# Swapping PSUM banks each step in latent attention, and a second expert unit ahead of the routes

## The reference

```python
logits = jnp.einsum('bsh,eh->bse', x, classifier_w)
probs = jax.nn.softmax(logits, axis=-1)
_, idx = jax.lax.top_k(probs + e_score_correction_bias, TOP_K)
rw = jnp.take_along_axis(probs, idx, axis=-1) * SCALE
w_full = jnp.sum(jax.nn.one_hot(idx, total) * rw[..., None], axis=-2)
act = jax.nn.silu(g) * u                      # g, u: each expert's gate and up products
expert_out = jnp.einsum('bsei,ehi->bseh', act, down_w)
out = jnp.einsum('bse,bseh->bsh', w_full[..., :n_routed], expert_out)

q_big = _apply_rope(jnp.einsum('bshk,hkq->bshq', q_hk, w_kc_q), sin_q, cos_q)
q_r = jnp.einsum('bshq,hqr->bhsr', q_big, W_qr)
k_r = jnp.einsum('bld,hdr->bhlr', kv_r, W_kr)
attn = jax.nn.softmax(jnp.einsum('bhsr,bhlr->bhsl', q_r, k_r), axis=-1)
ctx_c = jnp.einsum('bhsl,bld->bhsd', attn, kv_r)
```

## Time and profile before

| | |
|---|---|
| time, median of 3 runs | 873.98 us (868.6 to 875.28) |
| profiled execution | 870.11 us |
| its span, first to last instruction | 868.2 us |
| mean granted TensorE clock | 0.967 of full |
| TensorE matmul busy | 773.2 us (89%) |
| VectorE busy | 649.5 us (75%) |
| GpSimd busy | 553.4 us (64%) |
| ScalarE busy | 400.4 us (46%) |
| experts' first gate matmul | 191.70 us |
| latent attention's first query matmul | 377.37 us |
| last layer's first matmul | 769.4 us |

### The profile page before, as it was taken

One profiled execution on the slowest core, in us unless ns is written; L12 is line 12 of the kernel. 1 busy time (PEld: TensorE's weight loads), 2 busy tenths in 40 slices (PEclk: granted clock), 3 DMA queues, 4 the chain that ended last, 5 costly groups with the idle time before them and its releaser, 6 DMA issues. The chain is left out here.

```text
span 868.2 us, 14841 instructions
## 1 busy us (share of the span) xinstructions
PE 773.2 (89%) x4808; PEld 540.7 (62%) x4808; DVE 649.5 (75%) x1156; ACT 400.4 (46%) x1074; POOL 553.4 (64%) x545
## 2 busy tenths in 40 slices
PE   3999999686999999779999999999999999856785
PEld 1545455254878787666777777777777777533454
DVE  4888898467788787756656686978697669659994
ACT  2678787542222223224445444454444444443453
POOL 3555556423766666645566778787878787525985
PEclk9999999978999999989999999999999999997999
DMA  9200000003000001041210000000000000000001
GB/s 255 94 2 0 0 0 1 1 22 140 19 19 19 18 18 54 0 146 46 91 48 1 1 1 1 1 2 2 1 1 2 1 1 2 1 1 6 25 31 37
DMA packets 8762, 24.12 MB, mean 28 GB/s; under 512 B 1711, under 2 KB 5167, under 8 KB 8087
## 3 DMA queue, kind: packets, MB, share of 16 engines
q1 hardware_dynamic: 8154, 23.28, 8.2%
q10 hardware_dynamic: 549, 0.08, 0.1%
HBM read 21.26 MB, written 2.10 MB: 27 GB/s over the span
## 5 line engine op out<-in xcount | busy, mean ns | idle before, releaser
L1457 POOL TENSOR_TENSOR q<-turned 64x512 f32<-64x512 f32 x128 | 168.0, 1313 | 27.8 <-DVE turned L1381 10.7
L1144 PE MATMUL ps<-l_yt,a 128*128 128x512 f32 x576 | 150.5, 407 | 0.4 <-DVE l_yt L1346 0.4
L1144 PEld LDWEIGHTS ps<-l_yt,a 128*128 128x128 f32 x576 | 104.7, 191 | 32.2 <-DVE turned L1381 7.5
L1278 ACT ACTIVATE p<-ps,l_negmax 128x128 f32<-128x128 f32 x256 | 91.1, 383 | 59.8 <-DVE l_negmax L1372 59.8
L1444 POOL TENSOR_TENSOR p<-p,l_inverse 128x512 f32<-128x512 f32 x64 | 67.0, 1047 | 80.2 <-DVE l_inverse L1403 80.0
L1381 DVE TENSOR_TENSOR turned<-ps,rope 128x1024 f32<-128x1024 f32 x64 | 78.0, 1219 | 37.1 <-PE ps L1144 28.9
L765 PE MATMUL ps<-yt_experts,wsplit 128*128 (+1 forms) x384 | 95.9, 398 | 4.8 <-DVE h L854 3.0
L394 DVE TENSOR_REDUCE negmax<-ps 128x4 f32<-128x512 f32 x128 | 85.4, 688 | 11.0 <-PE ps L243 9.1
L765 PEld LDWEIGHTS ps<-yt_experts,wsplit 128*128 128x128 f32 x384 | 69.7, 188 | 21.8 <-issue 4.2
L325 ACT ACTIVATE pt<-ps 128x512 f32<-128x512 f32 x128 | 72.7, 596 | 7.6 <-PE ps L263 3.5
L1393 DVE TENSOR_TENSOR turned<-ps,rope 64x512 f32<-64x512 f32 (+1 forms) x96 | 65.6, 683 | 2.4 <-PE ps L1144 1.1
(11 more groups left out here) (188 smaller groups left out, 1604.4 us busy)
## 6 DMA issues: line engine op xcount, KB each, us to landing
wide<-in_wide SPq DMA_DIRECT2D x8, 768.0 KB, 4.3
mx_raw<-in_mx SPq DMA_DIRECT2D x8, 384.0 KB, 3.1
x<-in_x SPq DMA_DIRECT2D x4, 512.0 KB, 9.0
ctx_t<-in_ctx_t SPq DMA_DIRECT2D x1, 2048.0 KB, 7.8
out<-x SPq DMA_DIRECT2D x16, 128.0 KB, 1.7
narrow<-in_narrow SPq DMA_DIRECT2D x8, 192.0 KB, 2.6
ktraw<-in_ctx_rows SPq DMA_DIRECT2D x1, 1248.0 KB
wraw<-in_gate SPq DMA_DIRECT2D x1, 1024.0 KB, 18.6
```

The costliest lines, as they stand in the source:

```text
L1144: out = pe.matmul(tile_ps[t % 2], a[i][:, pa, kin, k * 128:(k + 1) * 128], yt[j % 2][:, py, kin, :, :].rearrange("p b s -> p (b s)"), star ...
L1278: t = act.activation(p[:, head, s, :], s_ps[head][:, s * S:(s + 1) * S], ACT.Exp, bias=negmax[:, head, s:s + 1], accum_out=total[:, head, ...
L1457: t = pool.tensor_tensor(out[rows[(head + half) % 2], head, :], turned[rows[head], half, :], turned[rows[head], 2 + half, :], ALU.add)
```

## The change

In latent attention banks 0 and 2 change roles every step. Tile 0 of step n goes to one of them, tile 2 to the other, tile 1 always to bank 1. The scores of head 0 share the bank of tile 2, and head 0's turned probabilities that of tile 0; head 1 keeps bank 3. Tile 2's wait on the rotation of tile 0 goes, and in its place it waits for the exponentials of head 0 of step n - 2. `turn_p` of head 0 and `score` get one more wait each, on the rotation of tile 0 of the loop they run in. Tile 0 waits for the rotation of tile 2 of the step before.

In the experts stage the routes no longer stand between step 0 and step 1: the gate and up products of unit 1 come before the wait for the routes. The weights of groups 0 and 1 are turned right behind them, into banks 6 and 7, those of groups 2 and 3 in steps 2 and 3, into bank 7, which they share with the chunks of L791. `quantise` is cut in two: `shift_up` (three operations) stands where it stood, `shift_down` (two) behind the addition of L865.

```diff
@@ routed_experts
+        weights_turned_ps = [m.bank(k)[0:WROWS, :] for k in (6, 7, 7, 7)]
         @block.tensor
-            def routes():
-                pe.wait_ge(route, ROUTE_STEPS)
-                for g in range(GROUPS):
-                    wait(pe, w_lo, g - 1)
-                    for s in range(4):
-                        t = pe.transpose(m.bank(6 + g % 2)[0:WROWS, s * S:(s + 1) * S], weights[:, 4 * g + s, :],
-                                         m.ident[:, :])
-                    t.then_inc(w_turned, 1)
-                pe.wait_ge(w_lo, GROUPS)
-                pe.wait_ge(m.selected, 1)
+            def routes(g):
+                if g == 0:
+                    pe.wait_ge(route, ROUTE_STEPS)
+                if g == 2:
+                    pe.wait_ge(w_lo, 2)
+                if g == 3:
+                    pe.wait_ge(mx_kept, 1)
+                for s in range(4):
+                    t = pe.transpose(weights_turned_ps[g][:, s * S:(s + 1) * S], weights[:, 4 * g + s, :], m.ident[:, :])
+                t.then_inc(w_turned, 1)
...
+                if isinstance(u, int) and u == 1:
+                    routes(0)
+                    routes(1)
+                    pe.wait_ge(w_lo, 1)
+                    pe.wait_ge(m.selected, 1)
+                if isinstance(u, int) and u in (2, 3):
+                    routes(u)
...
+                    if isinstance(u, int) and u in (2, 4):
+                        pe.wait_ge(w_lo, 2 + u // 2)
         @block.vector
                 if isinstance(u, int) and u == 0:
-                    routes()
+                    split_weights(0)
+                    split_weights(1)
+                if isinstance(u, int) and u in (2, 3):
+                    split_weights(u)
                 if inside(u, UNITS):
-                    (quantise if x % 2 else block_powers)(u, j, x)
+                    (shift_up if x % 2 else block_powers)(u, j, x)
...
                     dve.tensor_tensor(group, group, down_ps, ALU.add).then_inc(x_made, 1)
+                if x % 2 and inside(u, UNITS):
+                    shift_down(u, j, x)
@@ latent_attention
-        tile_ps, s_ps, proj_ps = [m.bank(0), m.bank(1)], [m.bank(2), m.bank(3)], m.ps[:, 4:6, :]
+        changing, proj_ps = [m.bank(0), m.bank(2)], m.ps[:, 4:6, :]
+        tile_bank = lambda n, k: (changing[n % 2], m.bank(1), changing[(n + 1) % 2])[k]
+        scores_bank = lambda n, head: (changing[(n + 1) % 2], m.bank(3))[head]
+        turned_p_bank = lambda n, head: (changing[n % 2], m.bank(3))[head]
...
-                    wait(pe, tile_turned, t - 1)
+                    if k == 2:
+                        if n == 0:
+                            pe.wait_ge(c_lo, 1)
+                        wait(pe, exp_made[0], n - 1)
+                    else:
+                        wait(pe, tile_turned, t - 2 * k)
...
                     pe.wait_ge(normed[head], n + 1)
+                    if head == 0:
+                        pe.wait_ge(tile_turned, min(TILES * (n + 2) + 1, TILES * STEPS))
...
                     pe.wait_ge(qs_made, n + 1)
+                    pe.wait_ge(tile_turned, min(TILES * (n + 1) + 1, TILES * STEPS))
```

More of the change, by code:

```diff
@@ L713, in group @@
                     step(EXPERTS * j + x, j, x)
-                    if isinstance(j, int) and x == 0:
-                        routes()
             group(0)
@@ L798, in _, with keep_weights @@
             t.then_inc(logits_turned, 1)
-            steps(pe, step, routes)
+            steps(pe, step)
         @block.scalar
         def _(act):
[L803 to L806, removed]
+            def keep_weights(g):
+                act.wait_ge(w_turned, g + 1)
+                act.activation(weights_t[:, g, :], weights_turned_ps[g], ACT.Copy).then_inc(w_hi, 1)
             def step(u, j, x):
@@ L813, in step @@
                     act.activation(gated[par][:, :], gate_ps[par], ACT.Silu).then_inc(gated_made, 1)
+                if isinstance(u, int) and u == 1:
+                    keep_weights(0)
+                    keep_weights(1)
+                if isinstance(u, int) and u in (2, 3):
+                    keep_weights(u)
                 if inside(u - 1, UNITS):
@@ L825, in _ @@
             act.activation(r.e[:, :, :], r.biased[:, :, :], ACT.Exp).then_inc(exp_made, 1)
-            steps(act, step, routes)
+            steps(act, step)
         @block.vector
@@ L835, in then, with split_weights @@
                 dve.wait_ge(route, count[0])
[L837 to L841, removed]
+            def split_weights(g):
+                dve.wait_ge(w_hi, g + 1)
+                dve.tensor_tensor(weights_t[LO:2 * LO, g, :], weights_turned_ps[g][LO:2 * LO, :],
+                                  weights_t[LO:2 * LO, g, :].bitcast(F32), ALU.subtract).then_inc(w_lo, 1)
             def step(u, j, x):
@@ L900, in quantise, with shift_down @@
                 then(2, dve.tensor_scalar(power[:, :], power[:, :], 1.0, None, ALU.max))
-                then(3, dve.scalar_tensor_tensor(out=shifted[:, :], in0=power[:, :], scalar=big, in1=w,
+                then(3, dve.scalar_tensor_tensor(out=shifted[:, :], in0=power[:, :], scalar=ROUND, in1=w,
                                                  op0=ALU.mult, op1=ALU.add))
-                then(4, dve.scalar_tensor_tensor(out=w, in0=power[:, :], scalar=-big, in1=shifted[:, :],
+            def shift_down(u, j, x):
+                c, w = 4 * j + x // 2, raw[(x // 4) % 2][:, (x // 2) % 2, :]
+                then = lambda k, instruction: mx_then(instruction, c, k, SCALE_STEPS)
+                then(4, dve.scalar_tensor_tensor(out=w, in0=power[:, :], scalar=-ROUND, in1=shifted[:, :],
                                                  op0=ALU.mult, op1=ALU.add))
@@ L1198, in score @@
                                 wait(pe, p_kept[head], n)
-                            t = pe.matmul(s_ps[head][:, s * S:(s + 1) * S], qs[rows[head], s * S:(s + 1) * S],
+                            t = pe.matmul(scores_bank(n, head)[:, s * S:(s + 1) * S], qs[rows[head], s * S:(s + 1) * S],
                                           m.keys[rows[head], 4 * (n // PAIRS) + s, :], start=True, stop=True)
@@ L1301, in keep_p @@
                     wait(act, ctx_made, n)
[L1302 to L1305 removed]
+                    act.activation(pt[:, head, :], turned_p_bank(n, head), ACT.Copy).then_inc(p_kept[head], 1)
+            keep_queries_weights(0, 0, m.bank(0))
+            keep_queries_weights(0, 1, m.bank(1))
             keep_rows(0, 0, w_ps)
             keep_rows(0, 1, q_ps)
[L1308 to L1309 removed]
+            keep_context_weights(0, m.bank(2))
+            keep_narrow_weights(0, m.bank(3))
             for n in RUN:
```

39 lines of the change are left out of this document (17 added, 22 removed).

## The result

| | before | after |
|---|---|---|
| median of 16 runs each | 873.01 us (865.86 to 875.51) | 863.87 us (858.79 to 869.11) |
| ratio to before, 95% interval | 1 | 0.9916 (0.9894 to 0.9938) |
| profiled execution, its span | 870.11, 868.2 us | 862.74, 860.8 us |

The account below looks back on a forecast made before the run. TensorE was taken to bound latent attention, busy 261.10 of 261.10 us, with real stalls in the experts stage. Gains of 3.4 + 2.6 + 2.2 = 8.2 us from a median of 873.98 gave 865.8 us, range 859 to 871.

Parts of the forecast that it names:

- Part 1: Latent attention: tile 2's new bank removes its late wait for tile 0's rotation, gaining 3.4 us, bounds 0 to 7.5.
- The rival that the spacing belongs to the bank: Latent loops: tile 2's spacings stay 0.32 and 0.34, owed to bank or stationary operand; 869.2 us, chance 0.17.
- The usual loops: Latent attention: 16 loops in which tile 2's two spacings shrink by 0.20 us together, 3.2 us in all.
- The four thin loops: Latent loops 10, 14, 22 and 30: VectorE's lateness leaves little cover, so 0.05 us gained each instead of 0.20.
- The rival in which the exponentials set tile 2: Latent loops: head 0's exponentials come too late and TensorE waits in every loop; 886 us, chance 0.05.
- Part 2: Experts' groups: shift_down behind the addition to x lets the down product start earlier; 2.6 us, bounds 1.5 to 4.8.
- The terms 0.6, 1.6 and 0.6: Gains in us forecast for units 10, 18 and 26 of the experts, 2.8 together, rounded down to 2.6.
- The term of 1.0 us for GpSimd's neighbourhood: Unit 18: moved behind the addition, L903 starts after GpSimd's L948 has ended, saving VectorE 1.0 us.
- Part 3: Start of the experts: unit 1's products fill TensorE's stand before the routes; 2.2 us gained, bounds 0.9 to 5.1.
- the clock's term: Unit 2 of the experts: half clock reaches into it, losing 1.2 us, half of the 2.5 if all ran so.
- those for a right forecast: Latent loop 10.88 us, spacings 0.23, no rotation or addition waits, shorter units 10, 18, 26, earlier unit 4, half clock past 205.7.
- the marks for a wrong forecast: TensorE waiting for L1278, a latent loop that stays at 11.09 us, or unit 2 beginning after 206.5.

Follow-up runs that it names:

- experiment four: Changed kernel with tile 2 made to wait for the rotation of tile 0 again, banks staying as changed; 865.32 us in a single run.
- Experiment six: Changed kernel with VectorE's four normalisations of rows before each late loop divided over two loops; 862.41 us, 0.9899 of the kernel before.
- experiment three: Kernel before with only shift_down moved behind the addition to x; 870.07 us, ratio 1.0008.
- Experiment seven: Changed kernel without VectorE's wait for its own last rounding operation, L927; 864.81 us, 0.9916 of the kernel before.
- Experiment five: Changed kernel with useless matmuls filling TensorE's two stands around the routes; 863.36 us, 0.9899 of the kernel before.
- experiment one: Kernel before with only the latent attention's part of the change; 868.16 us, ratio 0.9975.
- two: Kernel before with only the changed start of the experts, shift_down directly behind shift_up; 869.8 us, ratio 0.9985.
- ten: The changed kernel measured once more without any edit; 864.05 us, 0.9932 of the kernel before.

## Why the prediction came out right, and where not

**Part 1, 3.4 us: right in mechanism and size; measured 3.5.** The rival that the spacing belongs to the bank falls with experiment four. The usual loops gained more than the step said, 0.26 instead of 0.20: 0.21 in the two spacings, and most of the rest in the four matmuls behind them, whose spacings went from 0.236 on average to 0.227 (loop 10.82, forecast 10.88). The four thin loops gained nothing: the step said 0.05 each, and they lost 0.09. The step for them saw the right loops and the right releaser, the exponentials, with 0.13 us of cover in the earlier trace rows; it failed in the size of what the shorter loop takes away. The exponentials came 3.01 us into loop 14 instead of 2.75, later by all of the 0.26 that the loop before had become shorter: VectorE's four normalisations of rows in that loop are 1.25 us each, and they don't shorten. Experiment six gives back exactly these four loops. Between the starts of loops 8 and 31 lie 15 of the 16 usual loops: 15 x 0.26 - 4 x 0.09 = 3.5. The rival in which the exponentials set tile 2 is thus true in 4 loops of 24, and there it costs 0.36 us each.

**Part 2, 2.6 us: mis-sized; measured 1.2 in units 10, 18 and 26 (1.3 in units 4 to 31 of experiment three).** The terms 0.6, 1.6 and 0.6 measured 0.0, 1.1 and 0.1. That VectorE's work up to h has the same sum was right; that its order costs nothing was the step that failed. L927 is now followed at once by inner, which waits 0.57 us (unit 10), 0.34 (unit 18) and 0.33 (unit 26) behind it for VectorE's own signal; before, the addition stood there and the wait was 0.17. Why the same signal costs 0.17 us in one place and up to 0.57 in another stays open. Experiment seven takes this stand away and brings units 10 and 26 to a gain of 0.49 and 0.45, close to the 0.6 forecast. The term of 1.0 us for GpSimd's neighbourhood was right in the kernel after: its L925 in unit 18 took 0.55 us for the 1.54 of the earlier trace rows. The working let L903 end with GpSimd's L948; by its own numbers it ended 0.42 us later. By the Trainium skill, SBUF — State Buffer, section "SBUF: two separate sides", whichever of the two starts first, a VectorE operation with two inputs in SBUF or a GpSimd one, holds the port pair for its whole instruction. Experiment seven agrees: moving VectorE's work by some tenths let GpSimd's L970 start 0.08 us before L918, which then ended 0.41 us after it (289.29 and 288.88), for the same 1.0 us.

**Part 3, 2.2 us: measured 1.5, less 0.5 in the units behind.** The order of events was right: the routes end as before, and unit 2 begins 205.23 - 191.25 = 13.98 us after the first product, where unit 1 began 206.22 - 191.70 = 14.52 after it, 0.54 ahead (forecast 0.5). The half clock fell late and reached past 205.7, as forecast. Its term was mis-sized: I took half a unit, 1.2 us, and it covered the whole of unit 2. Experiment five, at full clock, has this unit in 5.99 us, so the clock's term is 2.03. The upper end of 2.5 was in the working; the middle was a choice. How much of it is the change's own, the other profiles show. With TensorE's old order the half clock reached into a unit in one of three: unit 1 took 4.62 us before, 4.58 in experiment one and 7.05 in three. With the new order and no useless products it did so in all six: unit 2 took 8.02 us (after), 8.00 (two), 7.65 (four), 8.21 (six), 6.92 (seven) and 7.00 (ten). So a loss of 0.9 to 2.2 us against the 5.99 comes with the new order, and its size is chance; from the first product to unit 4 these six take 25.83 to 27.38 us, 1.1 to 2.6 less than before. The 0.5 lost behind lies in units 4 and 5, for which the working had no term; it let units 2 and 3 alone take something back.

**The sum, 8.2 us: right as a number, better than its terms.** Where the change works, the trace shows 3.5 + 1.5 + 0.7 = 5.7 us (the 0.7 is part 2's 1.2 less part 3's 0.5), with 1.7 more elsewhere in the span, which is the clock's and chance. Medians gave 9.1 us in one set of runs and 5.5 in another. Both the 865.8 and "within 1%" hold, but that 8.2 lies so near to 9.1 is partly luck. The range held because its width came from the spread of the same kernel's runs.

**The marks.** Of those for a right forecast, four came in: the loop's period, the spacings, the lost line for the rotation, and a half clock past 205.7. Unit 18 moved, by 1.1 us of its 1.6, units 10 and 26 hardly did, and two of the three waits for the addition stayed, 1.4 us of 4.8. Unit 4 began at 218.19 us (191.25 + 26.94), 1.9 us before 220.1 and 1.5 when both are counted from their first product: just short of 2 to 3.5. Of the marks for a wrong forecast one came in: TensorE waits for the exponentials (L1278, now L1313), in four loops.

## What to carry to other kernels

A wait that comes late by a tenth of a microsecond in front of a weight load costs some 0.25 us each time, also in an engine that is 100% busy: look at the spacing of single matmuls, not at the idle time. When such a wait is removed, look for the few loops in which the new releaser comes from an engine with extra work, since they pay back, and spread that work. And before a gain of a few us in a program with idle stands is believed or denied, read its stages at the same granted clock; where a stand can be filled with useless products, the unit behind it cost 1 to 2 us less here, but they must be done before what TensorE waits for is ready, or they hold it up (1.0 us in experiment five).

## What was not expected of the hardware

The same kernel differs by about 0.33 us for each us at half clock, which varies from 45 to 75 us between runs. Such a stretch can be longer by 6.8 us while TensorE has the same instructions in the same order (the kernel before and experiment three). Latent loops 0 and 1 take 21.6 us with none on them, 23.2 with 3.4 us of it and 24.3 with 6.8, over all thirteen profiles. VectorE's own signal, when the very next instruction waits for it, made it stand 0.33 to 0.57 us behind an operation of 0.36. And a single f32 `SCALAR_TENSOR_TENSOR` of 128 x 384 takes 0.56 us or, with GpSimd at work, 1.54 to 1.62.
